# One scratch area for the experts' sums, with scatters in one chain, in a transformer layer with 64 experts

## What is computed

```python
x = x + layernorm(attn(layernorm(x)))
x = x + layernorm(ffn(layernorm(x)))
# attn: cq = h@Wc+bc; q = [cq@Wcq, rope(cq@Wqr)]; ckv = h@Wckv+bckv; k = [ckv@Wck, rope(h@Wkr)]; v = ckv@Wv+bv
scores = einsum('bsid,bsjd->bsij', q, k) * SCALER      # 16 x 16 per token
# ffn: E = 64, K = 6, CAP = 128, H = 512, I = 192
scores = softmax(xf @ gate_w.T); topk_w, topk_idx = top_k(scores, K)
gx = xp[buf_tok]                                        # the first 128 tokens of each expert
g, u = split(einsum('ech,ehi->eci', gx, gate_up_proj))
eo = einsum('eci,eih->ech', silu(g) * u, down_proj) * buf_w[..., None]
routed = zeros.at[buf_tok.reshape(-1)].add(eo.reshape(-1, h))
shared = silu(xf @ shared_gate_w.T) * (xf @ shared_up_w.T) @ shared_down_w.T
return routed + shared
```

## Time and profile before

| | us |
|---|---|
| median of 3 runs | 1913.72 |
| their range | 1912.94 to 1927.52 |
| the profiled execution | 1907.77 |
| its span | 1906.0 |
| mean granted clock | 0.968 of full |

### The profile page before, as it was taken

How to read it: one execution, slowest core, us unless ns; L and a number is a source line. 1 busy time by engine, 2 the same in 40 slices (tenths; PEclk the granted TensorE clock), 3 DMA queues, 4 the chain that set the end, 5 groups by cost and what they waited for, 6 DMA issues and landing times. The chain is left out here.

```text
span 1906.0 us, 48898 instructions
## 1 busy us (share of the span) xinstructions
PE 1769.8 (93%) x14281; PEld 1418.7 (74%) x14281; DVE 1509.3 (79%) x3940; ACT 967.3 (51%) x2129; POOL 522.6 (27%) x773
## 2 busy tenths in 40 slices
PE   5799999999999999999999999965999999998986
PEld 4688888888888888888888888854545555556865
DVE  6699999999999999999999999964444445437977
ACT  4465666666666656565656565631222323323433
POOL 1021211212121212121212121111344444444767
PEclk8799999999999999999999999977999999999998
DMA  6356565656666665656665666565799999988996
GB/s 223 89 140 174 146 177 147 173 154 166 161 160 168 157 171 153 175 152 174 153 173 154 174 153 176 133 160 168 235 312 324 336 330 346 349 258 320 416 414 265
DMA packets 549276, 400.83 MB, mean 210 GB/s; under 512 B 424872, under 2 KB 433192, under 8 KB 549160
## 3 DMA queue, kind: packets, MB, share of 16 engines
q1 hardware_dynamic: 528672, 341.77, 60.0%
q0 software_dynamic: 14336, 35.66, 7.7%
q10 hardware_dynamic: 6208, 22.68, 3.2%
HBM read 249.24 MB, written 150.63 MB: 210 GB/s over the span
## 5 line engine op out<-in xcount | busy, mean ns | idle before, releaser
L942 POOL TENSOR_SCALAR ve<-mv 128x1 f32<-128x1 f32 x192 | 42.3, 220 | 920.3 <-DVE mv L759 920.3
L646 ACT COPY kT<-bank 48x256 f32<-48x256 f32 x384 | 231.4, 603 | 37.2 <-PE bank L465 29.4
L1158 PE MATMUL e_gu<-w,xgT 128*128 128x384 f32 x512 | 187.6, 511 | 12.0 <-DMA w<-w_ed 9.8
L646 ACT COPY qT<-bank 48x256 f32<-48x256 f32 x512 | 188.5, 368 | 12.9 <-PE bank L465 2.0
L472 PE MATMUL bank<-wgu,xfT 128*128 128x416 f32 x512 | 188.8, 369 | 5.9 <-ACT xfT L646 4.9
L473 PE MATMUL bank<-wgu,xfT 128*128 128x416 f32 x512 | 183.6, 359 | 0.0
L1323 DVE SCALAR_TENSOR_TENSOR tanh<-tanh,e_gu 128x192 f32<-128x192 f32 x64 | 22.7, 355 | 165.0 <-ACT tanh L1246 165.0
L1158 PEld LDWEIGHTS e_gu<-w,xgT 128*128 128x128 f32 x512 | 94.5, 194 | 70.5 <-issue 10.7
L1424 POOL DMA_INDIRECT acc_scratch<-eo,sidx x64 | 101.5, 1587 | 120.0 <-ACT eo L1242 102.9
L1181 PE MATMUL e_ps<-w,hidT 96*128 96x512 f32 x256 | 128.2, 624 | 1.5 <-ACT hidT L1234 0.9
L476 PE MATMUL bank<-wgu,xfT 128*128 128x416 f32 x512 | 120.8, 359 | 0.3 <-DVE xfT L768 0.3
(11 more groups left out here) (184 smaller groups left out, 4750.4 us busy)
## 6 DMA issues: line engine op xcount, KB each, us to landing
w<-w_eg SPq DMA_DIRECT2D x60, 768.0 KB
acc_scratch<-zero SPq DMA_DIRECT2D x130, 256.0 KB, 4.0
w<-w_ed SPq DMA_DIRECT2D x60, 384.0 KB
w<-acc_scratch SPq DMA_DIRECT2D x40, 512.0 KB, 14.5
xf_scratch<-xf SPq DMA_DIRECT2D x64, 288.0 KB, 2.1
xin<-x SPq DMA_DIRECT2D x64, 256.0 KB, 2.8
x_raw<-xt SPq DMA_DIRECT2D x64, 256.0 KB, 3.2
v_scratch<-v SPq DMA_DIRECT2D x64, 256.0 KB, 3.5
```

Of the source, the lines that this page charges most:

```text
L646: nc.scalar.copy(dst, src).then_inc(done.sem, 1)
L1158: last = nc.tensor.matmul(gu_ps[par], xgT[:, par, n, :], w1[:, place, n, :], start=(n == 0), stop=(n == KD - 1))
```

## The change

The experts' sums go to one area: each scatter waits for the scatter before it, whichever expert it was. The last stage reads one area and adds once. With it comes a set of other edits:

- An expert's weights are laid out by partition on the host and come in one DMA of 9216 bytes per partition, instead of two (6144 bytes on 128 partitions, 4096 on 96).
- Down is split in a part over 128 hidden features (two matmuls of 256 columns) and one over 64 (two matmuls, on the lower and on the upper half of the rows). DVE writes hid in two instructions.
- The two index matmuls become one of 131 columns.
- kT gets the layout of qT; all eight copies are on ACT. Scores have heads outside and tokens inside, so the maximum reads with a stride; v is laid out to fit, stored with 4 DMAs instead of 1, and earlier in SP's list.
- Zero fill of one area, for tile i-2 instead of i-5. Ranks are loaded at iteration NT instead of NT+2 (the second part stays at NT+3).
- ACT loads experts 0 and 1 in iteration NT+2 behind the copy of oT, and 2 and 3 in NT+3, instead of at the end of NT+1 and NT+2.
- The splits of six weight parts (7 to 12) move from DVE to POOL; the biases are loaded an iteration earlier.

```diff
-    acc_d = [nc.dram_tensor(f"acc_scratch{n}", (T + CAP, D), F32).ap() for n in range(2)]
+    acc_d = nc.dram_tensor("acc_scratch", (T + CAP, D), F32).ap()
...
+        w = sb("w", [P, NW, WE])
+            src = w_e[e * P:(e + 1) * P, :] if isinstance(e, int) else w_e[bass.ts(e, P), :]
+            sp.dma_start(w[:, place], src).then_inc(w_in[place].sem, 16)
...
-                if active(i - 5):
-                    for a in acc_d:
-                        sp.dma_start(rows(a, i - 5), zero[:, 0:D]).then_inc(acc_out.sem, 16)
+                if active(i - 2):
+                    sp.dma_start(rows(acc_d, i - 2), zero[:, 0:D]).then_inc(acc_out.sem, 16)
...
+                    dst = v_d[1 - par].rearrange("c (j t d) -> t c j d", t=B4, d=DH)
+                    for n in range(B4):
+                        sp.dma_start(dst[n], v[n:P:B4, :].rearrange("p (j d) -> p j d", d=DH)).then_inc(v_out.sem, 16)
...
-                    spread(by_token, b3, a_kT, 1, (0,))
+                    spread(kT, b3, a_kT, 1)
...
+                if isinstance(i, int) and i == NT + 2:
+                    act.wait_ge(pe_k.sem, pe_k.at(NT - 1))
+                    settle(act)
+                    for n in range(2):
+                        load_expert(act, n, n)
...
+                if isinstance(i, int) and i == NT + 3:
+                    for n in range(2, NW):
+                        load_expert(act, n, n)
...
-                    nc.vector.tensor_reduce(smax4[:, halves[0]], sp4[:, halves[0]], AX.X, ALU.max).then_inc(d_s.sem, 1)
+                    nc.vector.tensor_reduce(smax4[:, halves[0]], by_key[:, halves[0]], AX.X, ALU.max).then_inc(d_s.sem, 1)
...
+                    for n in ON_POOL:
+                        nc.gpsimd.tensor_tensor(w[:, 1, m, :], stage, w[:, 0, m, :].bitcast(F32),
+                                                ALU.subtract).then_inc(pool_lo, 1)
...
+                    down = w[:, (place - 1) % NW, WU:WU + D]
                     for n in range(2):
-                        last = nc.tensor.matmul(out_ps, hidT[:, n, :], w2[0:PI, (place - 1) % NW, n, :],
-                                                start=(n == 0), stop=(n == 1))
+                        nc.tensor.matmul(out_ps[:, n], hidT[:, 0, :], down[:, n * HD:(n + 1) * HD], start=True, stop=False)
+                    for n in range(2):
+                        half = slice(64 * n, 64 * n + 64)
+                        last = nc.tensor.matmul(out_ps[:, n], hidT[half, 1, :], w[half, (place - 1) % NW, WU + D:],
+                                                start=False, stop=True)
...
-                    nc.tensor.matmul(find_ps[par][:, 0:P], sel[:], of(rank, j + 4), start=True, stop=True)
-                    nc.tensor.matmul(find_ps[par][:, P:P + 3], sel[:], of(base, j + 4), start=True,
+                    nc.tensor.matmul(find_ps[par][:, 0:P + 3], sel[:], of(rank, j + 4)[:, 0:P + 3], start=True,
...
-                    act.wait_ge(added[1 - par].sem, added[1 - par].at(j - 1 - NW))
+                    act.wait_ge(added.sem, added.at(j - 1 - NW))
...
-            def add_first(g, n):
+            def add(g, n):
                 dve.wait_ge(p_sh.sem, p_sh.at(g * 2 + n))
                 dve.wait_ge(acc_in[g % NA].sem, acc_in[g % NA].at(g))
-                nc.vector.tensor_tensor(sh_ps[n], sh_ps[n], acc[g % NA][:, n * D:(n + 1) * D], ALU.add).then_inc(v_y.sem, 1)
-
-            def add_second(g, n):
-                dve.wait_ge(v_y.sem, v_y.at(g * 2 + n, 1))
-                nc.vector.tensor_tensor(acc[g % NA][:, n * D:(n + 1) * D], sh_ps[n],
-                                        acc2[g % NA][:, n * D:(n + 1) * D], ALU.add).then_inc(v_y.sem, 1)
+                y = acc[g % NA][:, n * D:(n + 1) * D]
+                nc.vector.tensor_tensor(y, sh_ps[n], y, ALU.add).then_inc(v_y.sem, 1)
...
                     pool.wait_ge(ea_out.sem, ea_out.at(j - 1))
                     pool.wait_ge(ed_sidx.sem, ed_sidx.at(j - 1))
-                    pool.wait_ge(added[1 - par].sem, added[1 - par].at(j - 3))
+                    pool.wait_ge(added.sem, added.at(j - 2))
                     settle(pool)
-                    nc.gpsimd.indirect_dma_start(acc_d[1 - par], bass.IndirectOffsetOnAxis(
+                    nc.gpsimd.indirect_dma_start(acc_d, bass.IndirectOffsetOnAxis(
```

More of the change, by code:

```diff
@@ L252, in token_pipeline @@
         PART_AT = [-1] * 4 + [0] * 9 + [1] * 2
+        ON_POOL = range(7, 13)
         consts_in = sem("consts_in")
@@ L648, in iteration, with spread @@
             def iteration(i, par):
-                def spread(dst, src, done, n, pair=range(2)):
-                    for a in pair:
+                def spread(to, src, done, n):
+                    dst = to.rearrange("p c (m a) t -> p a m c t", a=2)
+                    for a in range(2):
                         sv = src[64 * a:64 * a + DQ, :].rearrange("p (m r c t) -> p r m c t", m=4, r=2, t=B4)
@@ L709, in iteration @@
                     copy(xT[:, 0].rearrange("p k t -> p (k t)"), x_raw[:, 1 - par, :], a_xT)
+                if isinstance(i, int) and i == -1:
+                    for dst, src in ((bq, b_q), (bck, b_ck), (bv, b_v), (bo, b_o)):
+                        act.dma_start(dst[:], src.partition_broadcast(P)).then_inc(biases_in, 16)
                 if isinstance(i, int) and i < 0:
@@ L747, in split @@
                 for n, (stage, w, m, _) in enumerate(parts):
-                    if PART_AT[n] == i:
+                    if PART_AT[n] == i and n not in ON_POOL:
                         dve.wait_ge(part_hi, n + 1)
@@ L1024, in experts_and_norm @@
         x_got = [count(f"x_got{n}", 16, NW, n) for n in range(NW)]
-        added = [count(f"added{n}", 16, 2, n) for n in range(2)]
+        added = count("added", 16)
         e_xT = count("e_xT")
@@ L1056, in experts_and_norm @@
         out_done = [ctx.enter_context(nc.semaphore(f"f_out{n}")) for n in range(NS)]
-        acc_in = [groups(f"f_acc_in{n}", 32, NA, n) for n in range(NA)]
+        acc_in = [groups(f"f_acc_in{n}", 16, NA, n) for n in range(NA)]
         p_hT = tiles("f_p_hT")
@@ L1106, in load_routed @@
             def load_routed(g):
-                for dst, a in zip((acc[g % NA], acc2[g % NA]), acc_d):
-                    sp.dma_start(dst, rows(group(a[0:T, :]), g)).then_inc(acc_in[g % NA].sem, 16)
+                sp.dma_start(acc[g % NA], rows(group(acc_d[0:T, :]), g)).then_inc(acc_in[g % NA].sem, 16)
             sp.dma_start(wsd_raw[:], w_sd.rearrange("(c p) n -> p c n", p=P)).then_inc(wsd_in, 16)
@@ L1119, in _ @@
             sp.wait_ge(wsd_lo, 1)
-            for n in range(2):
-                sp.wait_ge(added[n].sem, added[n].at(E - 2 + n))
+            sp.wait_ge(added.sem, added.at(E - 1))
             for g in range(NA):
@@ L1157, in iteration @@
                     for n in range(KD):
-                        last = nc.tensor.matmul(gu_ps[par], xgT[:, par, n, :], w1[:, place, n, :],
+                        last = nc.tensor.matmul(gu_ps[par], xgT[:, par, n, :], w[:, place, n * 2 * I:(n + 1) * 2 * I],
                                                 start=(n == 0), stop=(n == KD - 1))
```

175 lines of the change are left out of this document (78 added, 97 removed).

## The result

The changed kernel takes 1949.57 us (median of 4 runs, 1944.89 to 1956.94), beside 1913.33 of the kernel before: a ratio of 1.0184, 95% interval 1.0131 to 1.0238. It is slower beyond the noise, but not surely by 2%. The profiled execution is its fastest, 1944.89 us.

A forecast was written before the change was run, and what follows sets the result against it. PE was taken as full in token and last stages, PE and DMA both near full in the expert stage. +60 - 10 + 0 - 11 - 14 = +25 on 1906 gave 1931, stated as 1938 us among runs, range 1875 to 2015.

The forecast's parts named there:

- The chain: Expert stage: each scatter waits for the last one, so the pitch becomes 6.8 us, bounds 5.4 and 8.4; +60 us.
- the restart: Expert stage: time from a scatter's landing to the next issue, taken as 0.4 us from a gather following a copy.
- the straight line: Expert stage: landing interpolated between 5.04 us (empty DMA) and 8.0 (full), giving 7.5 at 82% of the DMA's work.
- the place of the weights' load: Expert stage: the load follows PE, so much falls after the landing, arguing for a landing of 5.0 to 5.5 us.
- The first rival: Expert stage: traffic hardly lengthens the landing, 5.4 us hides behind DMA's 5.45; stage -25, time 1854; chance 0.15.
- The third: Expert stage: the scatter chain stays at full load, pitch 8.2 us; +149 - 35, time 2028; chance 0.15.
- The second: Expert stage: the scatter chain is cut only to about 6.2 us; +23 - 35 = -12, time 1902; chance 0.25.
- Other expert edits worth nothing under the chain: Expert stage: shorter down and index matmuls cut PE from 5.6 to 5.0 us per expert, worth nothing at 6.8 pitch.
- Start and token stage: Start: 0, bounds -5 and +5. Token stage: kT copies shorten PE's wait before scores; -10 us, bounds -25 and +20.
- Between the stages: Between token and expert stages: moving four experts' weight loads shortens waits for oin and xf_scratch; -11 us, bounds -20 and 0.
- Last stage: Last stage: DVE waits less for scratch rows, group traffic falling from 2.49 to 1.97 MB; -14 us, bounds -22 and -5.
- What would show it: Expert stage signs: scatters over 6.4 us apart after idle on own DMA, PE busy near 75%, DMA share near 0.85.

The follow-up runs named there:

- two_chains: The changed kernel with two scratch areas again, each scatter waiting for the one before the last, two loads and adds in the last stage: 1852.28 us, ratio 0.9672.

## Why the prediction came out right

**The chain.** The mechanism was the right one and the size too small: +82 us instead of +60. The pitch was to be "issue to landing plus the restart", 6.4 + 0.4. The landing was 6.3 on average, so the 6.4 held, but partly by luck: it was the middle between two arguments (7.5 by the straight line, 5.0 to 5.5 by the place of the weights' load), and neither of the two came out. The restart is the term that was mis-sized: 0.85 us on average instead of 0.4, 63 x 0.45 = 28 us, and the shorter landing gives some 7 of them back. I took it from the gather that follows a DVE copy by 0.36 us. That is not what a scatter does after its wait, and the trace of before had a better row, in the chain, just ahead of the row of the last scatter:

```profile
1716.63 0.59 ACT eo L1242
1717.29 0.71 issue
1718.00 5.04 DMA acc_scratch<-eo,sidx
```

That wait was for ACT's copy and not for a landing, but the operation is the scatter: 0.71 us between the end of the wait and the issue, as also stand ahead of the last two scatters of the kernel after. What POOL does in it was not tried.

**The sum.** 1938 was said and 1949.57 measured. The chain was put 22 us too low, and the three other stretches gave 10 us more than was said, so two misses partly cancel.

**The first rival** (a landing that traffic hardly lengthens, 5.4 us a pitch) falls: even without any weights the landing is 4.8 in the median and the pitch 5.85. 5.4 is about the shortest of those 63 intervals (5.38), because of the same restart. The third (8.2 us) falls too: the traffic thins as the pitch grows (320 GB/s in the stage before, 261 after), and the time from issue to the last packet comes down from 7.8 us (median in the kernel before; the earlier trace rows is one of them) to 5.9. The second (6.2) would have wanted half the weights: that run had 6.38.

**How the landing falls with traffic** was argued by the load following PE "so much of it falls after the landing". The runs bear the direction out (moving the load nearer the scatter's start costs up to 0.41 us) but not the picture of a free place: in a chain a scatter is always under way, and the late prefetches lengthened the landings beside which they fell.

**Other expert edits worth nothing under the chain**: right, but for what the phase of the loads may give (7.14 against 7.52 with the old edits, above). PE's unhindered expert is 5.3 us and not 5.0:

```profile
1502.02 2.89 PE L1166 MATMUL e_gu<-w,xgT 128*128 128x384 f32 x8
...
1505.59 1.13 PE L1187 MATMUL e_out<-w,hidT 128*128 128x256 f32 x4
1506.65 0.70 PE L1190 MATMUL e_out<-w,hidT 64*128 64x256 f32 x4
1507.18 0.22 PE L1196 MATMUL e_find<-all_ranks,sel 64*128 x1
1507.33 2.85 PE L1166 MATMUL e_gu<-w,xgT 128*128 128x384 f32 x8
```

The first four records of down take 1.06 us to the next start, 0.265 each where I had 0.21. The second four, on 64 rows and as many columns, take 0.53, half of that: the pairs do run side by side. Where the chain does not bind, the stage was to be 343 us; two_chains has 348.

**Start and token stage**: -10 predicted, -17.6 measured. Of it 2.9 us lie ahead of tile 11, where I took 0 with bounds of 5 either way. From there it is 0.35 us a tile, 20.3 us by tile 62, and tile 63, which comes 21.5 us after tile 62, gives 2.6 of them back; why is open. The wait named was the right one, 7.2 us in front of the scores over 26 tiles. In the kernel after it is gone from the list, and PE is busy 498.5 of 500 us. I took 10 of the 18 us that it makes over 64 tiles, for fear of oin; PE's wait for oin is now 1.0 us in 27 tiles. The maximum's strided read was covered, and needed no cover: the two reduces take 689 and 681 ns, 683 before.

```profile
L858 DVE TENSOR_REDUCE smax<-score_ps 128x32 f32<-128x512 f32 x27 | 18.6, 689 | 0.3
L859 DVE TENSOR_REDUCE smax<-score_ps 128x32 f32<-128x512 f32 x27 | 18.4, 681 | 0.0
```

That the layout of kT made the gain, and not v's earlier stores, was not separated; that it is not the engine was.

**Between the stages** (-11, measured -12.8): the move of the four experts' loads is worth 5 to 8 of it by the run that undid it. **Last stage** (-14, measured -14.5): right in size, and in cause by the tiles of the two traces: the late tiles between 34 and 52 are gone, 12 us between the first tile and the last, and the rest is the first tile, which comes 10.1 us after the last scatter instead of 12.6. **What would show it**: the intervals are put down to the scatter's own DMA as named, but only 39 of the 63 are above 6.4 us, for at its shortest (5.5) a landing and the restart stay below it. The DMA share was to be near 0.85 and is 0.88, PE's busy share near 75% and is 80%.

## What to carry to other kernels

A serial chain of DMAs costs its landing under the load of the place, and the restart behind it; read both from a chain row of the same operation, not from another instruction of the engine, and compare their sum with the pitch that the rest can run at. If the sum is above it, the chain is the bound and every other saving in that stage is worth nothing: here the other edits were good for 20 us of the expert stage with two chains, and one wait hid them; the 30 us that the change gave ahead of the stage could not pay for it. Two chains had a landing half as long again (9.2 us against 6.2) at a shorter pitch.

## What the runs showed of the hardware that I had not expected

- An accumulating scatter of 128 rows of 2 KB, repeated in one chain, came every 5.6 us in the median (5.85 on average, never under 5.38) even with the DMA engines at a share of 0.59: a landing of 4.8 us and 0.8 us to the next issue.
- The time from a landing to the next issue was 0.80 to 0.89 us in 61 of 63 intervals of the kernel after, whether the landing took 4.7 or 9.4 us, and 0.80 in the median of all seven kernels with one chain.
- The same load of 1.18 MB lengthens the chain by 1.3 us where it starts with PE's end of an expert, and by 1.7 where it starts when a scatter has landed (PE's waits for it included).
- DVE's maximum over PSUM with a stride of 4 elements costs nothing (681 to 689 ns for 512 elements, 683 without), while a copy out of PSUM into kT's old layout costs 603 ns instead of 368 on ACT, and 601 instead of 427 on DVE.
- The mean granted clock is 0.92 in the expert stage of the kernel after and 1.00 in two_chains. Full is 2.4 GHz, and the 0.92 is made of 17 stretches at 1.2 GHz, 68 us in all, each of which follows an idle time of PE of 2 to 5 us. The scatter chain sets 61 of the 63 intervals there, so no time of the stage is put down to the clock.
